# Graph attention on one core: where the softmax sums are added up (accumulating DMAs take four of sixteen tiles, GpSimd six and their total, TensorE six in place of eight)

## The reference, cut to what matters

```
hs = layer_norm(relu(norm(x))); ht = layer_norm(h_target)
q, k, v = (ht @ Wq + bq) / sqrt(32), hs @ Wk + bk, hs @ Wv + bv
logits = where(edge_mask, q.k, -1e30)            # (8, 2048, 2048)
probs  = softmax(logits over the sources)
attn   = (probs @ v) @ Wo + bo
ht = layer_norm(ht + attn)
out = x + ht + gelu(ht @ W1) @ W2
```

## Time and profile before

| what | us |
|---|---|
| median of 3 runs | 495.03 (492.99 to 495.15) |
| the profiled execution | 494.16 |
| its span | 492.5 |
| busy: PE, DVE, ACT, POOL | 473.9, 419.1, 377.1, 305.4 |
| attention stage, first to last mask | 67.6 to 374.6 |

### The profile page before, as it was taken

One profiled execution on the slowest core, in us unless ns is written; L12 is line 12 of the kernel. 1 busy time (PEld: TensorE's weight loads), 2 busy tenths in 40 slices (PEclk: granted clock), 3 DMA queues, 4 the chain that ended last, 5 costly groups with the idle time before them and its releaser, 6 DMA issues.

```text
span 492.5 us, 10622 instructions
## 1 busy us (share of the span) xinstructions
PE 473.9 (96%) x4366; PEld 244.3 (50%) x4366; DVE 419.1 (85%) x631; ACT 377.1 (77%) x456; POOL 305.4 (62%) x152
## 2 busy tenths in 40 slices
PE   3999979999999999999999999999999999999995
PEld 1567523433333333333333333343434888888884
DVE  6889479999999999999999999999997977666343
ACT  4987968998998898998898998999995570727150
POOL 1000019996998999999999998999998300000000
PEclk9999989999999999999999999999999999999999
DMA  8997789723543674222772400070000100202021
GB/s 232 266 219 124 186 249 402 236 44 63 200 74 44 67 171 79 44 46 46 82 179 50 83 2 3 12 207 1 2 2 1 46 28 17 87 1 85 1 85 45
DMA packets 53774, 46.92 MB, mean 95 GB/s; under 512 B 35486, under 2 KB 46652, under 8 KB 53212
## 3 DMA queue, kind: packets, MB, share of 16 engines
q1 hardware_dynamic: 51216, 37.30, 28.3%
q0 software_dynamic: 2480, 8.92, 10.7%
q10 hardware_dynamic: 28, 0.01, 0.0%
HBM read 31.93 MB, written 14.81 MB: 95 GB/s over the span
## 4 chain that ended last, share of the span: by engine, by line
PE 61%; DVE 14%; issue 13%; ACT 5%; POOL 5%; DMA 1%; DVEq 0%; POOLq 0%
PE acc L1421 14%; PE slot L1406 13%; DVE probs L1032 10%; PE acc L1439 6%; PE slot L1521 3%; PE slot L1520 3%; PE slot L1519 3%; POOL added_up L547 3%; PE acc L1557 2%; PE acc L1558 2%; PE acc L1556 2%; PE slot L1472 2%; PE slot L1308 2%; DVE stats L852 1%; PE slot L1328 1%
## 5 line engine op out<-in xcount | busy, mean ns | idle before, releaser
L1032 DVE SCALAR_TENSOR_TENSOR probs<-maskT,slot 128x1024 f32<-128x1024 uint16 x256 | 298.4, 1217 | 8.1 <-PE slot L1406 7.8
L753 ACT ACTIVATE probs<-probs 128x1024 f32<-128x1024 f32 x256 | 267.0, 1057 | 25.7 <-DVE probs L1032 7.2
L547 POOL TENSOR_TENSOR added_up<-added_up,probs 128x1024 f32<-128x1024 f32 x96 | 226.7, 2417 | 1.0 <-ACT probs L753 0.9
L1421 PE MATMUL acc<-probs,V 128*32 128x512 f32 x1024 | 137.1, 607 | 1.0 <-ACT probs L753 1.0
L1439 PE MATMUL acc<-probs,ones 128*32 128x256 f32 x1024 | 77.1, 379 | 0.0
L1439 PEld LDWEIGHTS acc<-probs,ones 128*32 128x32 f32 x1024 | 33.3, 110 | 72.8 <-issue 71.2
L1406 PE MATMUL slot<-q_hi,k_hi 32*128 32x512 f32 x512 | 64.8, 496 | 3.8 <-DVE probs L1032 3.5
L544 POOL TENSOR_TENSOR added_up<-probs 128x1024 f32<-128x1024 f32 x16 | 38.1, 2411 | 29.4 <-ACT probs L753 18.8
L1406 PEld LDWEIGHTS slot<-q_hi,k_hi 32*128 32x128 f32 x512 | 24.6, 182 | 61.9 <-DVE probs L1032 55.2
L810 ACT ACTIVATE g_full<-slot 128x512 f32<-128x512 f32 x32 | 19.3, 602 | 45.2 <-issue 30.0
L1406 PE MATMUL slot<-q_lo,k_hi 32*128 32x512 f32 x512 | 52.0, 392 | 0.0
(11 more groups left out here) (142 smaller groups left out, 496.7 us busy)
## 6 DMA issues: line engine op xcount, KB each, us to landing
adj_raw<-in_adj POOLq DMA_DIRECT2D x16, 512.0 KB, 5.4
htn<-in_L_gnn_h_target SPq DMA_DIRECT2D x4, 512.0 KB, 5.7
ht_saved<-htn SPq DMA_DIRECT2D x1, 2048.0 KB, 6.8
k_hi_saved<-k_hi SPq DMA_DIRECT2D x1, 2048.0 KB, 10.6
k_lo_saved<-k_lo SPq DMA_DIRECT2D x1, 2048.0 KB, 14.1
v_saved<-V SPq DMA_DIRECT2D x1, 2048.0 KB, 9.0
inverse<-inverse_saved SPq DMA_DIRECT2D x8, 256.0 KB
maskT<-in_L_gnn_W SPq DMA_DIRECT2D x2, 1024.0 KB, 12.3
```

Of the source, the lines that this page charges most:

```text
L547: nc.gpsimd.tensor_tensor(added_up[:, pair], added_up[:, pair], at(i), ALU.add).then_inc(added, 1)
L753: nc.scalar.activation(p, p, ACT.Exp).then_inc(exped, 1)
L1032: nc.vector.scalar_tensor_tensor(out=probs[:, u % RING], in0=m, scalar=-HALF_EDGE, in1=slot[u % SLOTS][:], op0=ALU.add, op1=ALU.min).then_ ...
L1421: mm = pe.matmul(acc[HD * j:HD * j + HD, 0, :], V[:, i, h * HD:(h + 1) * HD], probs[:, (PAIRS * k + j // 2) % RING, j % 2, :], start=(i == 0),
```

## The change

What it does, in five parts. (1) Of the 16 tiles of a group, 0, 1, 5 and 8 (`GATHERED`) are added by DMAs in SBUF: ACT issues a plain copy of tile 0 into `gathered_up`, POOL then issues DMAs with an adding destination for tiles 1, 5 and 8, each after the one before has landed. POOL adds tiles 2, 3, 6, 10, then `gathered_up`, then 12 and 14 (6 adds per pair, 12 a group). PE takes six tiles. (2) PE's half sums are laid out by a table, at most one half per tile, starting at tile 3; the close comes as two halves, at tiles 1 and 2 of the next group, and after the last group it stands behind the first three products of `attend(2)`. (3) `gathered_up` lies in the rows 8 to 15 of `htn`; SP brings them back from `ht_saved` in the last group, and POOL makes chunk 2's residual only then, behind its last add. (4) POOL's other steps move behind the issue of the first gathers of the next group; the low part of W1 moves into the last group, behind its second round of adds. (5) ACT casts W1 and W2 in eight pieces, one every five units, loads the Gelu table before the last copy of the sums, and copies sums after unit 7. DVE's wait for `used` is gone: the ring's places come free by `begun`, `gathered` and `added`, and for PE's tiles by `scored`.

```diff
-    ADDED = [0, 1, 3, 5, 7, 9, 11, 13]
-    TAKEN = [i for i in range(ST) if i not in ADDED]
+    GATHERED = [0, 1, 5, 8]
+    ADDED = [2, 3, 6, 10, None, 12, 14]
+    TAKEN = [i for i in range(ST) if i not in ADDED and i not in GATHERED]
+    QUARTERS = [2, 2, 2, 0, 2, 2, 0, 2, 2, 2, 2, 2, 2, 2, 2, 2]
+    FIRST = 3
+    QUARTER = CHUNK // 4
...
+        SPARE = slice(2 * TILES, 4 * TILES)
+        gathered_up = htn[:, SPARE, :].rearrange("p t d -> p (t d)").rearrange(
+            "p (a b n) -> p a b n", a=PAIRS, b=2)
...  # SP, in the last chunk, after store_sums(c, 0)
+                if c == LAST:
+                    sp.wait_ge(ht_kept, 16)
+                    sp.wait_ge(added, (NCH * GROUPS - 1) * OPS + ADDED.index(None) * PAIRS)
+                    sp.dma_start(htn[:, SPARE, :], ht_saved[:, SPARE, :]).then_inc(ht_again, 16)
...  # POOL
+            def gather(G, i, pair):
+                k = G * ST + i
+                pool.wait_ge(exped, k * PAIRS + pair + 1)
+                if i == GATHERED[1]:
+                    pool.wait_ge(begun[pair], 16 * (G + 1))
+                else:
+                    pool.wait_ge(gathered[pair], gathered_through(k, pair) - 16)
+                pool.dma_start(gathered_up[:, pair], probs[:, (k * PAIRS + pair) % RING], accum_op=ALU.add
+                               ).then_inc(gathered[pair], 16)
...  # add_up(G, n, pair), the entry None
+                if i is None:
+                    pool.wait_ge(gathered[pair], 16 * (len(GATHERED) - 1) * (G + 1))
+                    nc.gpsimd.tensor_tensor(total, total, gathered_up[:, pair], ALU.add).then_inc(added, 1)
...  # POOL's round; behind() holds divide and make_residual
+                    for pair in range(PAIRS):
+                        gather(G, GATHERED[1], pair)
+                    if G:
+                        behind((G - 1) // GROUPS, (G - 1) % GROUPS)
+                    for n in range(1, len(ADDED)):
                         for pair in range(PAIRS):
-                            add_up(c, g, i, pair)
+                            add_up(G, n, pair)
+                        if n in (1, 2):
+                            for pair in range(PAIRS):
+                                gather(G, GATHERED[n + 1], pair)
...
+            behind(LAST, 1)
+            make_residual(2, 0)
+            make_residual(2, 1)
...  # ACT, after the exponentials of units 1 and 2 of a group
+            def begin_gathering(G, pair):
+                u = G * UG + GATHERED[0] * PAIRS + pair
+                act.wait_ge(exped, u + 1)
+                if G == 0:
+                    act.wait_ge(ht_kept, 16)
+                else:
+                    act.wait_ge(added, (G - 1) * OPS + (ADDED.index(None) - 1) * PAIRS + pair + 1)
+                act.dma_start(gathered_up[:, pair], probs[:, u % RING]).then_inc(begun[pair], 16)
...  # DVE, before it overwrites a unit
-                    dve.wait_ge(used, previous + 1)
-                    if place(previous)[2] in ADDED:
+                    if place(previous)[2] == GATHERED[0]:
+                        dve.wait_ge(begun[u % PAIRS], 16 * (previous // ST + 1))
+                    elif place(previous)[2] in GATHERED:
+                        dve.wait_ge(gathered[u % PAIRS], gathered_through(previous, u % PAIRS))
+                    elif place(previous)[2] in ADDED:
...  # PE
+            def sum_weights(G, at, tiles=range(len(TAKEN) + 1)):
+                visit = (at - FIRST) % ST
+                begin = sum(QUARTERS[(FIRST + v) % ST] for v in range(visit))
+                end = begin + QUARTERS[at]
+                for n in tiles:
+                    low, high = max(begin - 4 * n, 0), min(end - 4 * n, 4)
+                    if low < high:
+                        sum_part(G, n, low, high)
```

More of the change, by code:

```diff
@@ L249, in graph_attention @@
         exped = sem("exped")
-        used = sem("used")
         added = sem("added")
+        begun = [sem(f"begun{pair}") for pair in range(PAIRS)]
+        gathered = [sem(f"gathered{pair}") for pair in range(PAIRS)]
         context_done = sem("context_done")
@@ L580, in _ @@
[L580 to L589 removed]
+                    G = c * GROUPS + g
@@ L1425, in weigh, with sum_part @@
                     mm.then_inc(context_done, 1)
-                elif i in ADDED:
-                    mm.then_inc(used, 1)
-            def sum_weights(k, half):
-                c, g, i = place(k)
-                G = c * GROUPS + g
-                ts = slice(half * CHUNK // 2, (half + 1) * CHUNK // 2)
-                first = i == TAKEN[0]
-                if first and G and not half:
+            def sum_part(G, n, low, high):
+                ts = slice(low * QUARTER, high * QUARTER)
+                last = n == len(TAKEN)
+                if last and low == 0:
+                    pe.wait_ge(added, OPS * (G + 1))
+                if n == 0 and low == 0 and G:
                     pe.wait_ge(sums_out, G)
                 for j in range(PER):
-                    mm = pe.matmul(acc[HD * j:HD * j + HD, 1, ts], ones[:],
-                                   probs[:, (PAIRS * k + j // 2) % RING, j % 2, ts],
-                                   start=first and not half, stop=False)
-                if half:
-                    mm.then_inc(used, 1)
-            def close(G):
-                pe.wait_ge(added, OPS * (G + 1))
-                for j in range(PER):
-                    mm = pe.matmul(acc[HD * j:HD * j + HD, 1, :], ones[:], added_up[:, j // 2, j % 2, :],
-                                   start=False, stop=True)
-                mm.then_inc(closed, 1)
+                    if last:
+                        weights = added_up[:, j // 2, j % 2, ts]
+                    else:
+                        weights = probs[:, (PAIRS * (G * ST + TAKEN[n]) + j // 2) % RING, j % 2, ts]
+                    mm = pe.matmul(acc[HD * j:HD * j + HD, 1, ts], ones[:], weights,
+                                   start=(n == 0 and low == 0), stop=last and high == 4)
+                if last and high == 4:
+                    mm.then_inc(closed, 1)
+            def sum_weights(G, at, tiles=range(len(TAKEN) + 1)):
[6 more added lines that the diff above has]
+                        sum_part(G, n, low, high)
             def attend(c, tiles=range(TILES)):
@@ L1484, in _ @@
                 weigh(k)
[L1485 to L1492 removed]
+                G = k // ST - (k % ST < FIRST)
+                if G >= 0:
+                    sum_weights(G, k % ST)
+            for at in range(FIRST):
+                sum_weights(NCH * GROUPS - 1, at, range(len(TAKEN)))
             def turn_y(c):
@@ L1570, in _ @@
             attend(2, [0, 1, 2])
+            for at in range(FIRST):
+                sum_weights(NCH * GROUPS - 1, at, [len(TAKEN)])
             turn_y(0)
```

103 lines of the change are left out of this document (58 added, 45 removed).

## The result

The changed kernel took 583.68 us (median of 4 runs, 570.89 to 590.72) against 495.04 for the kernel before on the same chip: a ratio of 1.161, with an interval of 1.151 to 1.171. The forecast was 494.3 and the range ended at 505. The profiled execution took 577.42 us, its span 575.8, which is 83.3 more than before.

What follows compares the result with a forecast made beforehand. VectorE was taken as the attention stage's bound, with 8.1 us of idleness. The terms -7.2 + 1.0 + 0.5 + 1.5 + 4.3 made +0.1 us on 494.16, forecast 494.3 us, no change; range 488.5 to 505.

Steps and rivals of the forecast that it cites:

- landings in a chain: Rival, chance 0.20: late gathers make GpSimd wait at successive places, the close then holding TensorE and VectorE; 500.8 us, or 524.
- Both signs of being wrong: Stated tests that would refute the forecast: gathers landing above 8 us, or an attention stage over 304 us.
- step 3: GpSimd's waits for copies and gathers in the attention stage: landings 5.0 and 7.6 us, only group 3 late, +1.0 us.
- the ring: Six tile places in the attention stage, each wanted by the sixth mask after; nothing late, tile 8 landed 31.5, wanted 33.8.
- step 1, -1.1: ScalarE's weight casts in eight pieces of about 0.5 us, partly absorbed between exponentials in the attention stage: -1.1 us.
- step 1, -6.1: TensorE's half sums in the attention stage: no tile has two, 15 doubles each give about 0.41 back, -6.1 us.
- step 6: The tail after the last mask: VectorE's third residual add waits for GpSimd's moved residual steps, first widening product +4.3 us.
- step 5: Group 0, where copies and gathers share the engines with SP's saves: between 0 and 5 us, taken +1.5.
- the rival of a dearer issue: Rival, chance 0.08: each gather costs GpSimd 1.0 us to issue in place of 0.57; 508 us.

Runs made afterwards that it cites:

- e2_plain: The changed kernel with GpSimd's gathers as plain copies instead of adding transfers, order and waits kept, sums wrong; 531.38 us.
- e3_no_turns: The changed kernel without the mask's transposing transfers of chunks 2 and 3, mask loads kept; 552.71 us.
- c2_casts: The kernel before with only ScalarE's two weight casts in four pieces each; 493.20 us.
- e1: The changed kernel without copies, gathers and the waits for them, tiles 0, 1, 5 and 8 missing from the sums; 507.63 us.
- e4_late_split: The changed kernel with the eight weight casts from unit 228, three units apart, instead of from 212, five apart; 563.14 us.
- t2_clean_order: The changed kernel without copies, gathers and the load returning ht rows, with casts from unit 228 and chunk 2's residual in groups 6 and 7; 493.29 us.
- c1_spread: The kernel before with TensorE's quarter sums spread, close over two tiles, sums copied later, casts in four pieces each, no wait for `used`; 497.29 us.
- t1_residual_last: The kernel before with only chunk 2's two residual steps moved behind GpSimd's last add; 498.82 us.
- t1b: The kernel before with chunk 2's residual steps behind GpSimd's last add and the norm's first small instruction as a scalar_tensor_tensor; 498.25 us.

## Why the prediction was wrong

The mechanism that decided is the rival *landings in a chain*. Its sign was right and, of its places, the waits at the gathers of tile 8 and at the add of the gathered rows. Both signs of being wrong that the prediction named came: gathers land above 8, and the stage took 378.2 us, not under 304. But the rival's price was 6.6 us, or 30 at worst, its chance 0.20, and the largest wait, VectorE's own for a place in the ring, was not in it.

1. *The landing of an adding transfer* (step 3) is the term that failed. "which is just what a mask load moves: 5.0 us quiet, up to 10.2 under load" was right for quiet ones: 4.6 to 5.9, and 7.2 to 8.7 for the second of a pair (forecast 7.6). It failed as an upper bound: twelve gathers took 9.5 to 20.6 us, where the bound was 10.2. The kernel before moved a stage's transfers with the engines busy 0.39 of the time, some 120 of 307 us; the 48 gathers and 16 copies alone added 138.5 and 23.6 us of all engines, together 282 or 0.92 of the old stage, and in the stage as it became the share was 0.80. I had counted the new transfers' landings but never their sum against the engines' spare time, and took a maximum of 10.2 from an emptier machine. e2_plain (-44) and e3_no_turns (-26) show two parts of it, which overlap: the adding, with its doubled engine time, and the meeting with transposes. What happens inside when they meet isn't settled: from about 206 to 214 us the engines are busy 0.27 of the time and move 64 GB/s while two gathers, a transpose and a mask load are under way, so it is no lack of bytes per second.
2. *Who waits* (step 3). The prediction checked the ring for landings on time only, and priced a late one by the close alone. It reaches VectorE directly, through the ring of six tiles: 44.1 us in ten waits. The margins worked out there (tile 8 landed at 31.5, wanted at 33.8) were 2 us wide for a transfer whose own bounds, 3.9 and 10.2, were 6 apart.
3. *ScalarE's casts* (step 1, -1.1). Pieces do help (c2_casts: VectorE's idle pieces -0.6, time -1.6). What the prediction passed over is that the first piece now stands at unit 212, eight units ahead, while W1's load waits for SP's sums of the group before: 14.3 us of wait in the changed kernel, 6.6 in e1 with no gather about. e4_late_split gives 19 us back.
4. *TensorE's relayout* (step 1, -6.1). Only in t2_clean_order can it be seen: -3.8 for the whole stage with no gathers. The pieces at the doubled halves are gone there as forecast, but four of GpSimd's six later rounds now come at tile 10 and behind, and the close waits for the last (0.6 to 0.8 at five closes). The wait for the close was forecast at 1.0 in all, for group 3 alone. c1_spread shows that smoothing without taking work off TensorE saves 1.8 and costs 4.1 by the later close.
5. *The tail* (step 6, +4.3). Its timing of GpSimd was right: residual steps end 16.6 us after the last mask (forecast 16.0). The path was wrong. It was not VectorE's residual add that waited for GpSimd's result. Small instructions of the norm, ahead of it in VectorE's order, stood through GpSimd's last adds and both residual steps, and the widening came at 26.8 instead of 19.0. Of the 12.1 us against before, 10.3 lie ahead of the scaling by the norm, and 1.8 behind it, where TensorE's granted clock was 0.69 after its wait, and 1.00 before. t1_residual_last shows it by itself: +4.0 us in a kernel where by my steps the move costs nothing. The Trainium skill, "SBUF — State Buffer", section "SBUF: two separate sides", says that the pair of ports which VectorE and GpSimd share is an exclusive lock: a VectorE instruction in a mode of two ports or with two inputs in SBUF, and a GpSimd instruction, block each other fully, and the first to start has the pair for the whole instruction. The trace agrees as far as each held instruction ended with one of GpSimd's. It goes beyond it with the 8.38 us, since here the ends of three adds passed without VectorE being let in. No run looks at the lock itself.
6. *Group 0* (step 5, +1.5). The place was named, with 0 to 5 us; VectorE's waits for gathers there sum to 12.8. Its copies took 10.7 to land and its gathers up to 17.0.
7. *Right:* the issue. A gather shows 0.94 us of busy time at the median (0.85 to 2.15), but GpSimd's next instruction starts 0.57 after it (202.46 to 203.03), so the rival of a dearer issue is refuted. The copies landed in 3.3 at the median (taken: 3.9) and ScalarE's issues took 0.47. No run looks at the close in two halves behind `attend(2)` or at the earlier Gelu table by themselves.

## What to carry to other kernels

Before a transfer inside SBUF replaces arithmetic, add up its engine time over the stage and compare it with the spare time of the DMA engines; here the sum was 0.92 of the stage, under one, and still too much. An adding transfer cost twice a copy here (2.9 against 1.4 us of all engines for 512 KB). A margin in a ring must hold the landing beside the worst neighbour. When a large GpSimd instruction is moved, look at which small VectorE instructions now run beside it: work that seems covered on another engine isn't if VectorE stands still while it runs. And spare time on the average is worth nothing to a chain of adds whose inputs come late; look at when each input is ready.

## What the runs showed of the hardware

- Adding transfers and transposing ones delay each other: the two transposes that held SP's queue for 6.5 and 6.7 us before held it for 15.4 and 13.2 beside gathers (7.1 and 6.4 in e1, without gathers), and the gathers landed in 14.5 to 20.6 instead of 5 to 9.
- VectorE instructions of 128x4 that read SBUF were held until a GpSimd instruction with two inputs in SBUF ended, in three forms: tensor_scalar (8.38 us here, 8.95 in e4), scalar_tensor_tensor (1.31, t1b), tensor_tensor (2.18, e1); unhindered they take 0.16 to 0.17. VectorE's masks, which read scores from TensorE's accumulators, kept their 1.216 us beside the same adds.
- How long such a hold lasts is not only the rest of one GpSimd instruction. In e1 and t1 VectorE was let in at the end of each. In the changed kernel GpSimd's instructions overlap by 0.3 us in the trace (one add starts at 450.49, the one before ends at 450.79), in e1 by 0.04, and VectorE got in only at 459.99, where there was a gap. Whether the overlap is the cause isn't shown.
- TensorE's granted clock fell with the waits. From 459.3 to 469.5 it was 0.50, its lower level of 1.2 GHz: TensorE had been idle from 454.4 but for the close of 1.1 us, stayed idle until 465.7 and was busy again for the rest; then 1.00. For the whole changed kernel it was 0.928 against 0.995, and the page's row of tenths shows 5 or 6 in the slices with the longest waits.
- The lower level costs VectorE time once more. Behind the hole of 9.76 us at 161.3 the clock was 0.50 until 169.1, and a tile's product with V took 1.93 us, then 1.07:

```profile
165.32 1.93 PE L1502 MATMUL acc<-probs,V 128*32 128x512 f32 x8
...
169.42 1.07 PE L1502 MATMUL acc<-probs,V 128*32 128x512 f32 x8
```
VectorE waited another 0.63 and 1.76 us for scores there. Pieces of 1.3 to 1.8 stand in the same way behind four other holes, and are part of the 14.8 us of small waits named above.
